# First and second product between two graph layers taken by units of ten columns, with the last two units' evictions on ScalarE

## What is computed

```python
h = relu(layernorm(x))                                   # layer 0
msg = relu(h[src] + (edge_attr @ W_edge.T + b_edge))
h = (1 + eps) * h + segment_sum(msg, dst)
x = x + relu(h @ W1.T + b1) @ W2.T + b2                   # first and second product
h = relu(layernorm(x))                                   # layer 1
m = relu(h[src]) + 1e-7
a = softmax of m over the edges of each dst
x = x + (h + segment_sum(a * m, dst)) @ W + b
```

## Time and profile before

| | us |
|---|---|
| median of 3 runs | 2431.22 |
| the profiled execution's own time | 2425.77 |
| its span | 2424.0 |
| end of layer 0's last sum, first matmul of the first product | 2008.5 |
| last second product summed into xs | 2043.1 |
| first matmul of the long run of block products (line 864) | 2085.1 |
| end | 2424.0 |

### The profile page before, as it was taken

How to read it: one execution, slowest core, us unless ns; L and a number is a source line. 1 busy time by engine, 2 the same in 40 slices (tenths; PEclk the granted TensorE clock), 3 DMA queues, 4 the chain that set the end, 5 groups by cost and what they waited for, 6 DMA issues and landing times.

```text
span 2424.0 us, 54194 instructions
## 1 busy us (share of the span) xinstructions
PE 1792.9 (74%) x11221; PEld 1480.3 (61%) x11222; DVE 1891.8 (78%) x4571; ACT 762.8 (31%) x1322; POOL 1731.9 (71%) x1796
## 2 busy tenths in 40 slices
PE   3778777767676766777666767676776766899999
PEld 2466665656555555656555656565555654688887
DVE  8999998878787787887887878887888888454544
ACT  5001112222323333334444444444455556000000
POOL 4777777777777777777777777777777770477774
PEclk9899898988888888888888888888888887999999
DMA  5133444444434445454444445545554444877774
GB/s 165 42 94 91 110 102 104 123 105 113 126 102 124 122 108 137 111 140 127 123 136 128 132 130 139 139 130 137 137 137 136 138 127 142 314 264 270 264 273 149
DMA packets 172472, 344.69 MB, mean 142 GB/s; under 512 B 72689, under 2 KB 126763, under 8 KB 158078
## 3 DMA queue, kind: packets, MB, share of 16 engines
q1 hardware_dynamic: 33378, 153.14, 21.5%
q0 software_dynamic: 60864, 99.55, 17.4%
q10 hardware_dynamic: 77990, 89.82, 10.9%
HBM read 247.65 MB, written 94.68 MB: 141 GB/s over the span
## 4 chain that ended last, share of the span: by engine, by line
POOL 57%; issue 19%; PE 15%; DVE 2%; DMA 2%; ACT 1%; SPq 0%; POOLq 0%; DVEq 0%; ACTq 0%
POOL rows_buf L598 57%; PE ps L864 11%; PE ps L874 2%; DMA rows_buf<-table,index 1%; ACT features_buf L947 0%; PE ps L887 0%; PE ps L679 0%; PE ps L794 0%; DMA final<-residual 0%; DVE ps L1350 0%; PE ps L848 0%; SPq L535 0%; DVE zone L1387 0%; PE ps L881 0%; DMA table<-features_buf 0%
## 5 line engine op out<-in xcount | busy, mean ns | idle before, releaser
L598 POOL DMA_INDIRECT rows_buf<-table,index x1539 | 1493.7, 971 | 495.3 <-issue 492.6
L794 PE MATMUL ps<-zone,planes 128*128 128x400 f16 x2352 | 614.4, 377 | 538.4 <-DVE zone L1387 436.2
L1005 ACT ACTIVATE features_buf<-ps 128x800 f16<-128x800 f32 x392 | 327.8, 836 | 1216.0 <-PE ps L794 1211.1
L1387 DVE TENSOR_SCALAR zone<-iota_c,planes 128x400 f16<-128x400 int16 x2352 | 664.7, 336 | 57.6 <-issue 47.6
L794 PEld LDWEIGHTS ps<-zone,planes 128*128 128x128 f16 x2352 | 250.1, 106 | 715.3 <-issue 657.4
L679 PEld LDWEIGHTS ps<-wet,zone 128*128 128x128 f32 x3136 | 544.9, 248 | 43.6 <-issue 32.5
L679 PE MATMUL ps<-wet,zone 128*128 128x96 f32 x3136 | 531.9, 328 | 8.1 <-DMA zone<-edge_t 8.1
L666 PE MATMUL ps<-onehot,features_buf 128*96 128x128 f32 x3120 | 425.4, 282 | 0.0
L666 PEld LDWEIGHTS ps<-onehot,features_buf 128*96 128x96 f32 x3120 | 392.2, 173 | 11.1 <-issue 0.7
L1350 DVE TENSOR_TENSOR ps<-ps,rows_buf 128x768 f32<-128x768 f32 x171 | 164.6, 962 | 244.1 <-DMA rows_buf<-table,index 216.8
L1148 DVE TENSOR_TENSOR planes<-ps,planes 128x1536 f16<-128x1536 f32 x196 | 341.5, 1742 | 0.0
(11 more groups left out here) (187 smaller groups left out, 785.5 us busy)
## 6 DMA issues: line engine op xcount, KB each, us to landing
counts<-features_buf ACTq DMA_DIRECT2D x392, 200.0 KB
zone<-edge_t SPq DMA_DIRECT2D x98, 768.0 KB
single<-table SPq DMA_DIRECT2D x3072, 0.4 KB
rows_buf<-counts SPq DMA_DIRECT2D x24, 1600.0 KB
rows_buf<-table,index POOLq DMA_INDIRECT x1539
planes<-counts SPq DMA_DIRECT2D x12, 1600.0 KB
table<-planes SPq DMA_DIRECT2D x5, 840.0 KB
final<-residual ACTq DMA_DIRECT2D x48, 48.0 KB
```

What stands on the lines that cost most here:

```text
L598: nc.gpsimd.indirect_dma_start(out=into[:, t, :], out_offset=None, in_=table, in_offset=bass.IndirectOffsetOnAxis(ap=at[:, t:t + 1], axis= ...
L794: nc.tensor.matmul(count_ps[:, bass.ds(banks[k], WC)], row_hot[:, u % 2, g * GS + k, :], pair_hot[:, g * GS + k, :], start=False, stop=Fal ...
L1005: nc.scalar.activation(count_out[:, k], bank, ACT.Copy, accum_out=row_sum[:, bass.ds(p, 1)]).then_inc(moved, 1)
L1387: last = nc.vector.tensor_scalar(pair_hot[:, k, :], iota_c[:, :], step_pair[:, bass.ds(i * (IS * SC) + (u * SC + k), 1)], None, ALU.is_equal)
```

## The change

- The first product goes by units of ten columns: three pieces of 4, 4 and 2 columns (500, 500 and 250 nodes), read from `acc` by column, into two PSUM banks by turns. The output is by column, so the evictions write `uT` side by side.
- The second product of unit u follows the first product of unit u+1 on PE, in banks 2 and 3. The order on PE, with the last `count_steps` in it, is written out.
- DVE evicts units 0 to 2, ACT units 3 and 4, after its last `close` and ahead of `deviation_of(1, 0)`. DVE evicts unit 2 after the moments of unit 0.
- The reductions of the count sums go behind the moments of unit 1, the operations that set `fast` and `block_edges` behind those of unit 3, and `block_start` behind the last unit. `count_checks(0)` on PE goes behind the second product of unit 3, the matmul for `block_start` behind that of unit 4.
- ACT's wait for the stored counts goes behind `deviation_of(1, 1)`, SP gets the same wait ahead of `block_load(0)`, and ACT reads the flag one unit later.

```diff
-UC = 250
-UP = UC // NJ
-HB = 4
+PIECES = ((0, 4), (4, 4), (8, 2))
+HU = 3
...
+        def hidden_piece(u, k):
+            j0, n = u * UN + PIECES[k][0], PIECES[k][1]
+            return (uT[:, j0 * NP:(j0 + n) * NP], ps[0:D, (u * len(PIECES) + k) % 2, 0:n * NP])
...
+                for k in range(OB):
+                    sp.wait_ge(stored[k], (NPAIR // OB + 1) * 16)
                 block_load(0)
                 sp.wait_ge(starts_ready, 1)
...
-            for k in range(N // UC):
-                if k >= HB:
-                    pe.wait_ge(hidden_out, k - HB + 1)
-                nc.tensor.matmul(ps[0:D, k % HB, 0:UC], w1s[:, :], acc[:, 0, k * UC:(k + 1) * UC],
-                                 start=True, stop=True).then_inc(hidden_ps, 1)
-                if k % HB == HB - 1 and k // HB < GC:
-                    count_steps(NC - 1, NS - 1, k // HB, *last_steps[k // HB])
-
-            node_layer(hidden_out, N // UC, uT.rearrange("f (j p) -> f j p", j=NJ), w2s, 0)
+            def first_products(u):
+                for k, (j0, n) in enumerate(PIECES):
+                    piece = u * len(PIECES) + k
+                    if piece >= 2:
+                        wait_hidden(pe, piece - 1)
+                    nc.tensor.matmul(hidden_piece(u, k)[1], w1s[:, :],
+                                     by_column(acc[:, 0, 0:N])[:, u * UN + j0:u * UN + j0 + n, :],
+                                     start=True, stop=True).then_inc(hidden_ps, 1)
+
+            def second_products(u):
+                wait_hidden(pe, (u + 1) * len(PIECES))
+                for g in range(u * UN // JG, (u + 1) * UN // JG):
+                    if g >= 2:
+                        pe.wait_ge(node_out, g - 1)
+                    for k in range(JG):
+                        j = g * JG + k
+                        last = nc.tensor.matmul(ps[0:NP, 2 + g % 2, k * D:(k + 1) * D],
+                                                uT[:, j * NP:(j + 1) * NP], w2s[:, :], start=True, stop=True)
+                    last.then_inc(node_ps, 1)
...
+            first_products(0)
+            last_counts(0)
+            first_products(1)
+            second_products(0)
+            last_counts(1)
+            first_products(2)
+            second_products(1)
+            last_counts(2)
+            last_counts(3)
+            first_products(3)
+            second_products(2)
+            first_products(4)
+            second_products(3)
+            count_checks(0)
+            second_products(4)
+            count_checks(1)
...
-            for k in range(OB):
-                act.wait_ge(stored[k], (NPAIR // OB + 1) * 16)
-
+            for u in range(HU, NU):
+                hidden_of(u)
             deviation_of(1, 0)
             for u in range(1, NU):
                 deviation_of(1, u)
+                if u == 1:
+                    for k in range(OB):
+                        act.wait_ge(stored[k], (NPAIR // OB + 1) * 16)
                 if u < NU - 1:
                     feature(1, u - 1)
-                if u == 1:
+                if u == NU - 2:
                     flag = fast_of(act)
...
-            for k in range(N // UC):
-                if k == HB:
-                    pair_hots(NC // IS - 1, IS + NS - 1, GC - 1)
-                dve.wait_ge(hidden_ps, k + 1)
-                nc.vector.tensor_scalar(uT.rearrange("f (j p) -> f p j", j=NJ)[:, k * UP:(k + 1) * UP, :],
-                                        ps[0:D, k % HB, 0:UC].rearrange("f (p j) -> f p j", j=NJ), b1c[:, 0:1],
-                                        0.0, ALU.add, ALU.max).then_inc(hidden_out, 1)
+            hidden_of(0)
+            pair_hots(NC // IS - 1, IS + NS - 1, GC - 1)
+            hidden_of(1)
             dve.wait_ge(bias_added, NU)
...
             for u in range(NU):
                 for g in range(u * UN // JG, (u + 1) * UN // JG):
                     add_node(0, g)
                 dve.wait_ge(node_out, (u + 1) * UN // JG)
                 moments_of(1, u)
+                if u == 0:
+                    hidden_of(2)
                 if u == 1:
-                    dve.wait_ge(starts_ps, 1)
-                    nc.vector.tensor_copy(block_start[:, :], ps[0:1, 5, 0:NB]).then_inc(starts_ready, 1)
+                    dve.wait_ge(cleared, PB + NPAIR)
...
+                if u == 3:
+                    dve.wait_ge(bad_ps, 2)
...
                 if u:
                     scale_of(1, u - 1)
+            dve.wait_ge(starts_ps, 1)
+            nc.vector.tensor_copy(block_start[:, :], ps[0:1, 5, 0:NB]).then_inc(starts_ready, 1)
```

More of the change, by code:

```diff
@@ L305, in gnn_kernel @@
         hidden_ps = sem("hidden_ps")
-        hidden_out = sem("hidden_out")
+        hidden_out = [sem(f"hidden_out{k}") for k in range(2)]
         node_ps = sem("node_ps")
@@ L419, in gnn_kernel, with wait_hidden @@
         weighted, own_rows = table1.bitcast(F16), table0
+        def wait_hidden(engine, pieces):
+            on_dve = HU * len(PIECES)
+            engine.wait_ge(hidden_out[0], min(pieces, on_dve))
+            if pieces > on_dve:
+                engine.wait_ge(hidden_out[1], pieces - on_dve)
+        def hidden_piece(u, k):
+            j0, n = u * UN + PIECES[k][0], PIECES[k][1]
+            return (uT[:, j0 * NP:(j0 + n) * NP], ps[0:D, (u * len(PIECES) + k) % 2, 0:n * NP])
         def wait_high(engine, u):
@@ L688, in count_checks @@
                     nc.tensor.matmul(ps[0:NB, 7, 0:1], in_block[:, :], ones[:, 0:1], start=True, stop=True).then_inc(bad_ps, 1)
-                if g == 3:
+                if g == 1:
                     pe.wait_ge(edges_moved, 1)
@@ L844, in _, with last_counts @@
             pe.wait_ge(layer_summed, 1)
[L845 to L853 removed]
+            def first_products(u):
[16 more added lines that the diff above has]
+                    last.then_inc(node_ps, 1)
+            def last_counts(g):
+                count_steps(NC - 1, NS - 1, g, *last_steps[g])
+            first_products(0)
[14 more added lines that the diff above has]
+            count_checks(1)
             with pe.If(fast_of(pe) > 0):
@@ L1019, in _, with hidden_of @@
                     close(i * OB + k, k, needed[k])
-            for k in range(OB):
-                act.wait_ge(stored[k], (NPAIR // OB + 1) * 16)
+            def hidden_of(u):
+                for k in range(len(PIECES)):
+                    act.wait_ge(hidden_ps, u * len(PIECES) + k + 1)
+                    into, found = hidden_piece(u, k)
+                    nc.scalar.activation(into, found, ACT.Relu, bias=b1c[:, 0:1]).then_inc(hidden_out[1], 1)
+            for u in range(HU, NU):
+                hidden_of(u)
             deviation_of(1, 0)
@@ L1180, in add_node @@
                 part = xs[:, g * JG:(g + 1) * JG, :].rearrange("p j d -> p (j d)")
-                nc.vector.tensor_tensor(part, part, ps[0:NP, g % 4, 0:JG * D], ALU.add).then_inc(node_out, 1)
+                bank = g % 4 if layer else 2 + g % 2
+                nc.vector.tensor_tensor(part, part, ps[0:NP, bank, 0:JG * D], ALU.add).then_inc(node_out, 1)
             dve.sem_inc(acc_done, 2)
@@ L1446, in _, with hidden_of @@
             dve.sem_inc(layer_summed, 1)
-            for k in range(N // UC):
-                if k == HB:
-                    pair_hots(NC // IS - 1, IS + NS - 1, GC - 1)
-                dve.wait_ge(hidden_ps, k + 1)
-                nc.vector.tensor_scalar(uT.rearrange("f (j p) -> f p j", j=NJ)[:, k * UP:(k + 1) * UP, :],
-                                        ps[0:D, k % HB, 0:UC].rearrange("f (p j) -> f p j", j=NJ), b1c[:, 0:1],
-                                        0.0, ALU.add, ALU.max).then_inc(hidden_out, 1)
-            dve.wait_ge(bias_added, NU)
[L1456 to L1468, removed]
+            def hidden_of(u):
+                for k in range(len(PIECES)):
+                    dve.wait_ge(hidden_ps, u * len(PIECES) + k + 1)
+                    into, found = hidden_piece(u, k)
+                    nc.vector.tensor_scalar(into, found, b1c[:, 0:1], 0.0, ALU.add, ALU.max
+                                            ).then_inc(hidden_out[0], 1)
+            hidden_of(0)
+            pair_hots(NC // IS - 1, IS + NS - 1, GC - 1)
+            hidden_of(1)
+            dve.wait_ge(bias_added, NU)
             for u in range(NU):
@@ L1473, in _ @@
                 moments_of(1, u)
+                if u == 0:
+                    hidden_of(2)
                 if u == 1:
-                    dve.wait_ge(starts_ps, 1)
-                    nc.vector.tensor_copy(block_start[:, :], ps[0:1, 5, 0:NB]).then_inc(starts_ready, 1)
+                    dve.wait_ge(cleared, PB + NPAIR)
+                    nc.vector.tensor_reduce(bad[:, 2:3], row_sum[:, :], AX.X, ALU.max).then_inc(bad_ready, 1)
+                    nc.vector.tensor_reduce(in_block[:, :], row_sum[:, :].rearrange("p (b k) -> p b k", b=NB), AX.X, ALU.add
+                                            ).then_inc(bad_ready, 1)
+                if u == 3:
```

(11 more changed lines are left out.)

2 lines of the change are left out of this document (removed).

## The result

The changed kernel took 2459.29 us (median of 6 runs, 2456.47 to 2467.77) against 2433.65 for the kernel before in 6 runs: a ratio of 1.0117, 95% interval 1.0102 to 1.0132. The medians lie 25.6 us apart, the ratio says 28; both stand for the loss in what follows. The profiled execution took 2467.77 us with a span of 2466.0. Its layer 0 ended 10.5 us later than in the profile before (first matmul of the first product at 2019.06, not 2008.52), which the change does not touch; so dates are compared counted from that matmul.

What follows compares the result with a forecast made beforehand. The long run's start was taken to hang on SP's queue and the issue of `block_load(1)`: 13.4 us later, less 0.8 for a closed gap, +12.6 us on the median of 2431.22 gives 2443.8 us, range 2434 to 2452.

Steps and rivals of the forecast that it cites:

- What bounds the kernel: SP's queue: the issue of block_load(1) sets the long run's start, with 9.3 MB in 33.3 us ahead of the last own store.
- the price of the read: First product on PE: columns read 200 bytes apart at 1.09 ns each, so a unit takes 2.73 instead of 2.11 us.
- Rival 1: First product on PE: strided read costs as much as strided writes, a unit 4.2 us, total 2449.3 us; chance 0.27.
- the prediction's own bounds: PE's strided read in the first product: 0.84 ns a column at no loss, at most 2.0 as for ACT's write.
- The new wait: DVE, behind the moments of unit 1, waits for ACT's first root, free near 2027 until 2034.5: some 7 us.
- `block_start` last: Made after unit 4 at 2048.2, then 13 edge-list loads: block_load(1) at 2056.6 against 2043.15, 13.4 us later.
- The 0.8 us given back: Stretch of stores: the gap of 2055 to 2058 closes, 3 us at 220 instead of 304 GB/s, giving back 0.8 us.
- Rival 2: SP's queue runs faster when never short: 9.3 MB at 400 GB/s in 25 instead of 33.3 us, +5 us, 2436.5; chance 0.15.

Runs made afterwards that it cites:

- the read by itself: Separate kernel of matmuls alone, 96 rows by 500 columns, at several column distances: float32 pass 0.42 us side by side, 0.94 at 200 bytes.
- a free read: Changed kernel with the first product reading side by side, wrong nodes in each unit: 2440.95 us, 12.7 above the kernel before, ratio 1.0057.
- the last one: Changed kernel, strided read kept, with roots first, flag and block_start early, lists behind the last own store: 3882.58 us, 22.7 above the kernel before.

## Why the prediction was wrong

**What bounds the kernel: right.** The long run stayed 340 us long and moved with its start, and its start with SP's queue. `block_load(1)` followed the last addition by 11.4 us, forecast 11.3 (2.88 + 8.42). The stretch behind it took 35.2 and 32.4 us in the two profiles of the change, 33.3 and 33.2 in those of the kernel before.

**The first step that failed is the price of the read:** "The row nearest in kind is a read by PE: weights 100 bytes apart [...] at most 1.09 ns a column [...] I take 1.09". A moving operand read 200 bytes apart takes 1.88 ns a column. The weight load was the wrong neighbour: the read by itself shows float16 columns 100 bytes apart at 1.78 ns, where the weights 100 bytes apart had 1.09 at most. ACT's and DVE's writes, 2.0 ns, came nearest in size, though they are another engine's and nothing here shows a common cause. Rival 1 had the doubled read, at 0.27.

**The second is the clock, which no case held.** All prices of PE stood at the clock of before, without a reason given. It fell to half in the first product. In the chain that ended last, a unit of the second product takes 4.15 us, against 2.17 with the side-by-side read, and a group of counts 1.0, against 0.51 in the kernel before. Up to the root that is three units and four groups, 3 x 1.98 + 4 x 0.49 = 7.9 us, beside 6250 x 2 x 1.04 ns = 13.0 us for the read itself. Of these 20.9 us 15.3 arrive at the root (40.7 against 25.4 with the read taken back); the rest goes into waits that stand there without it. The read alone, 1.88 ns, lay inside the prediction's own bounds of 0.84 and 2.0. The time went out of the range by 7 us (2459 against 2452), and the clock is the term that the range did not have. It is also why rival 1's 2449 was too low.

**The new wait: right in place, too large in worth.** The forecast gave it some 7 us of DVE. DVE waited 11.5 us for the root; with the roots first the last addition came 3.3 to 5.9 earlier, part of that by the clock, since PE was needed for the rest.

**`block_start` last: right.** It is the larger part of the 12.7 us that stay with a free read: 11.5 us between last addition and `block_load(1)`.

**The 0.8 us given back: not shown.** The stretch of stores, forecast at 32.5 us, took 35.2 in the first profile of the change and 32.4 in the second; that scatter is larger than the term. Rival 2, a faster queue, did not happen: 306 and 309 GB/s with the stores ready.

**That moving the lists would free the queue** was held by no case in so many words, but the reading behind it, that all hangs on the issue of `block_load(1)`, was too simple: with the issue 11.4 us earlier 3.8 came through, and part of the rest was SP held at the lists while the transfer engines ran short.

Sum of the parts: of the 26 to 28 us read and clock make 13 to 15 by the times, the order of roots, flag and lists the other 13 or so. By themselves, with the rest of the order unchanged, read and clock cost 18 us in the old order and 20 in the last one.

## What to carry to other kernels

Before a kernel is reordered around a new operand, look at the distance between neighbouring elements in bytes. Here a read 200 bytes apart more than doubled the time of each pass, and the clock fell to half for the work behind it too. When work is pulled forward on one engine, follow the small things that are pushed back with it (here a flag and 49 numbers) to the queue that waits for them: 13 tiny loads, hidden by one microsecond before, held back 9 MB. And a saturated queue got shorter here by bytes taken out of it into an idle time (33 to 27 us); moving its head forward by 11.4 us brought 3.8, and small loads between large stores let the queue run short.

## What the runs showed of the hardware

- PE's read of the moving operand goes by bytes of distance: at a clock of 1.00 0.84 ns a float32 column side by side and nearly so at 8 bytes, 1.3 at 12, 1.76 at 16, 1.88 at 200; float16 0.42, doubled at 8 bytes, 1.8 from 16 on. The Trainium skill (SBUF — State Buffer, the note on cachelines) has distances up to four float32 or eight bfloat16 elements, 16 bytes, as free. The measurement differs: at that distance float32 costs a factor of 2 and float16, of the same size as bfloat16, a factor of 4.
- The time of such a read does not depend on the granted clock: 0.94 us a pass both at 1.00 (2020.00 to 2020.94) and at 0.50 (2055.11 to 2056.05). A side-by-side pass does: 0.42 us at 1.00, 0.83 at 0.50 (the float32 groups behind the strided ones). At half clock a read 16 bytes apart, 0.88, costs hardly more than that.
- The granted clock fell to 0.50 of 2.4 GHz in all float32 groups from 16 bytes on and stayed at 1.00 at 8 and 12; in float16 it fell from 8 bytes on and stayed at 4. PE shows as busy 100% in all of them. In the side-by-side groups behind them it came back.
- The same 13 small loads took SP's queue 6.9 us when it was empty and 21.2 us behind the stores. Some 5 MB were still queued when they began (an estimate: 7.1 MB issued from 2060.50 on, less what 308 GB/s moved by 2066.7). The median list took 0.43 us even there, the longest 6.7.
